# A list of 128 indices loaded as one run and turned onto the partitions by TensorE, with 2 MB instead of 1.5 MB of x loaded ahead of a gather

## The reference, cut to what matters

```python
# x: (128, 64, 512) float32, 16.8 MB
# itok_B_0_7: (128,) int32 in 0..7; itok_B_1_198: (128,) int32 in 1..198
# L0_cond_weights: (8, 64, 64); L1_cond_weights: (200, 64, 64)
w = L0_cond_weights[itok_B_0_7]
x = x + einsum('bct,bcd->bdt', x, w)
w = L1_cond_weights[itok_B_1_198]
x = x + einsum('bct,bcd->bdt', x, w)
return x
```

## Time and profile before

| | us |
|---|---|
| median of 3 runs | 92.57 (92.44 to 92.94) |
| the profiled execution | 92.7 |
| its span, first to last instruction | 90.8 |
| TensorE busy | 76.8 (85%) |
| VectorE busy | 60.0 (66%) |
| ScalarE busy | 57.0 (63%) |
| bytes moved by DMA | 35.93 MB, mean 396 GB/s |

### The profile page before, as it was taken

The page is one execution under the profiler, slowest core; times in us unless marked ns, Lnnn a source line. Parts: engine busy times, 40 slices in busy tenths (PEclk is TensorE's granted clock), DMA queues, the critical chain, the costliest instruction groups (busy, mean ns, idle before and its releaser), DMA issues.

```text
span 90.8 us, 2458 instructions
## 1 busy us (share of the span) xinstructions
PE 76.8 (85%) x906; PEld 42.9 (47%) x906; DVE 60.0 (66%) x124; ACT 57.0 (63%) x114; POOL 23.5 (26%) x119
## 2 busy tenths in 40 slices
PE   0599959977999999999999999999999999992000
PEld 0489749965545443544544454454444444440000
DVE  1096019994388787978878788888787887887000
ACT  2899807885367675867776677777576775775000
POOL 3400049989998988000000000000000000000000
PEclk9999999999999999999999999999999999999755
DMA  0999999999999999999999999999999999999992
GB/s 6 337 446 424 455 361 415 420 399 409 409 413 402 409 418 394 419 418 424 411 415 426 415 413 420 420 422 420 411 415 422 420 419 428 404 424 420 419 399 103
DMA packets 9453, 35.93 MB, mean 396 GB/s; under 512 B 737, under 2 KB 866, under 8 KB 9314
## 3 DMA queue, kind: packets, MB, share of 16 engines
q1 hardware_dynamic: 4512, 16.78, 46.1%
q10 hardware_dynamic: 4786, 16.91, 45.8%
q0 software_dynamic: 144, 2.10, 5.4%
HBM read 19.01 MB, written 16.78 MB: 394 GB/s over the span
## 4 chain that ended last, share of the span: by engine, by line
PE 68%; DMA 12%; DVE 9%; issue 1%; DVEq 1%; ACTq 0%; POOLq 0%
PE psum L225 58%; DMA w_rows<-in_L_cond_weights_dram,cond 10%; DVE w L269 7%; PE psum L206 7%; PE psum L247 2%; DMA subjects<-in_itok_B_dram 2%; DVEq L75 1%; PE psum L186 1%; DVE xy L303 1%; ACTq L370 0%; DVE m_diag L276 0%; DVE w_rows L365 0%; POOLq L155 0%; DVEq L275 0%
## 5 line engine op out<-in xcount | busy, mean ns | idle before, releaser
L225 PE MATMUL psum<-xy,m_diag 64*128 64x512 f32 x240 | 53.4, 595 | 0.0
L303 DVE COPY xy<-psum 64x512 f32<-64x512 f32 x60 | 41.0, 684 | 11.1 <-PE psum L225 10.2
L303 ACT COPY xy<-psum 64x512 f32<-64x512 f32 x60 | 34.9, 582 | 17.5 <-PE psum L225 16.8
L225 PEld LDWEIGHTS psum<-xy,m_diag 64*128 64x128 f32 x240 | 22.6, 187 | 25.6 <-issue 25.0
L163 POOL COPY w0b<-w0t 64x64 f32 x112 | 21.7, 237 | 10.1 <-DMA w_rows<-in_L_cond_weights_dram,cond 8.2
L206 PEld LDWEIGHTS psum<-w,w0b 64*32 64x32 f32 x512 | 5.6, 105 | 6.4 <-issue 3.0
L269 ACT COPY w<-psum 64x256 f32<-64x256 f32 x16 | 5.8, 365 | 3.8 <-PE psum L186 2.8
L186 PE MATMUL psum<-ident,w_rows 128*64 128x128 f32 x64 | 7.2, 274 | 1.0 <-DVE w_rows L365 1.0
L378 ACT COPY w<-w_rows 128x256 f32<-128x256 f32 x18 | 7.3, 405 | 0.8 <-DMA w_rows<-in_L_cond_weights_dram 0.2
L186 PEld LDWEIGHTS psum<-ident,w_rows 128*64 128x64 f32 x64 | 7.0, 151 | 1.3 <-DVE w_rows L365 1.3
L206 PE MATMUL psum<-w,w0b 64*32 64x64 f32 x512 | 6.9, 224 | 0.9 <-DVE w L269 0.9
(11 more groups left out here) (14 smaller groups left out, 7.2 us busy)
## 6 DMA issues: line engine op xcount, KB each, us to landing
xy<-in_x_dram SPq DMA_DIRECT2D x15, 1024.0 KB, 19.7
out_dram<-xy ACTq DMA_DIRECT2D x14, 1024.0 KB, 14.4
out_dram<-xy ACTq DMA_DIRECT2D x4, 512.0 KB, 8.3
xy<-in_x_dram SPq DMA_DIRECT2D x2, 512.0 KB, 5.8
w_rows<-in_L_cond_weights_dram ACTq DMA_DIRECT2D x1, 128.0 KB, 2.5
cond<-in_itok_B_dram SPq DMA_DIRECT2D x1, 0.5 KB, 2.2
subjects<-in_itok_B_dram ACTq DMA_DIRECT2D x1, 0.5 KB
w_rows<-in_L_cond_weights_dram,cond POOLq DMA_INDIRECT x1, 9.2
```

Source lines behind the costliest of these rows:

```text
L225: last = nc.tensor.matmul(psum[:, 2 * (s % Y_RING) + h, :], m_diag[rows, odd, v % M_RING, j, :], xy[rows, s, j * T:(j + 1) * T], start=j = ...
L303: copy(xy[rows, s, i * T:(i + 1) * T], psum[HALVES[i], 2 * (s % Y_RING) + h, :]).then_inc(done, 1)
```

## The change

The index list is loaded as one run of 512 bytes into one partition, `cond_row`. VectorE converts its 128 integers to floats, TensorE transposes the row of floats into a column of PSUM (128 partitions, one value each), and VectorE converts that column back to integers in `cond`, on which the gather waits. SP issues 2 MB of x instead of 1.5 MB before its wait, in two loads of 1 MB; the second was two loads of 0.5 MB, with the wait between them.

```diff
+        cond_row = sb("cond_row", [1, B], i32)
+        cond_float = sb("cond_float", [1, B], fp32)
         cond = sb("cond", [B, 1], i32)
...
+        cond_psum = psum[:, 6, 0:1]
...
-            sp.dma_start(cond[:, :], cond_dram.rearrange("(b o) -> b o", o=1)).then_inc(s_cond, 16)
+            sp.dma_start(cond_row[:, :], cond_dram.rearrange("(o b) -> o b", o=1)).then_inc(s_cond_row, 16)
             load(0, 2)
-            load(2, 1)
+            load(2, 2)
 
             sp.wait_ge(s_w0b_early, EARLY * UNIT)
-            load(3, 1)
             for v in range(2, UNITS):
                 load(2 * v, 2)
...
-            pool.wait_ge(s_cond, 16)
+            pool.wait_ge(s_cond, 1)
             nc.gpsimd.indirect_dma_start(
...
             pe.wait_ge(s_ident, 1)
+            pe.wait_ge(s_cond_float, 1)
+            nc.tensor.transpose(cond_psum, cond_float[:, :], ident[0:1, 0:1]).then_inc(s_cond_turned, 1)
+
             pe.wait_ge(s_w0_rows, 16)
...
-                    pe.wait_ge(s_x[v], 32 if v == 1 else 16)
+                    pe.wait_ge(s_x[v], 16)
...
+            dve.wait_ge(s_cond_row, 16)
+            nc.vector.tensor_copy(cond_float[:, :], cond_row[:, :]).then_inc(s_cond_float, 1)
+            dve.wait_ge(s_cond_turned, 1)
+            nc.vector.tensor_copy(cond[:, :], cond_psum).then_inc(s_cond, 1)
+
             dve.wait_ge(s_ident, 1)
             dve.wait_ge(s_subjects, 16)
             dve.wait_ge(s_w0_turned, 1)
```

More of the change, by code:

```diff
@@ L95, in bass_cond_residual_kernel @@
         w0_psum = psum[0:C, 7, :]
+        cond_psum = psum[:, 6, 0:1]
+        s_cond_row = sem("s_cond_row")
+        s_cond_float = sem("s_cond_float")
+        s_cond_turned = sem("s_cond_turned")
         s_cond = sem("s_cond")
```

## The result

The changed kernel takes 93.53 us (median of 6 runs, 93.15 to 94.34) against 92.70 (6 runs, 92.44 to 92.94). The ratio is 1.0105, with a 95% interval of 1.0058 to 1.0152: it is slower, by 0.8 us at the median. I had forecast no change, 92.6 in a range of 92.0 to 93.1. In what follows, four slow runs of the experiment e3 (94.06 to 94.54 us) are left out of its median and its ratio.

What follows compares the result with a forecast made beforehand. The prediction took the DMA engines to bind the kernel. Start 0.0, crossing 0.0 and TensorE 1.3 us later but hidden left the span at 90.8 us, a median of 92.6 us, range 92.0 to 93.1.

Steps and rivals of the forecast that it cites:

- the cover: At the last store: TensorE and the copies may come up to 3.1 us later before the end moves.
- Step 1: Load of the index list at the start: 0.0 us taken, bounds -0.74 and +0.16.
- Step 2: Chain from cond to the gather: gather starts at 3.85 instead of 3.26, 0.6 us later, hidden by x.
- Step 3: 0.52 MB more x ahead of the gather: 1.28 us more, gather lands at 13.7 instead of 12.42.
- Step 4: Work behind the gather: 1.3 us later, TensorE ends at 83.6, hidden by the cover of 3.1 us.
- third rival: TensorE becomes the bound, over 3.1 us late through its clock or shared engines: 94.4 or 93.9 us; chance 0.05.
- Step 5: Two 0.5 MB loads of x made into one of 1 MB, and three semaphores: costs nothing.
- second rival: Gather ready only after x is through at 8.0 us, engines idle: 0.1 to 0.7 us slower; chance 0.06.

Runs made afterwards that it cites:

- e3: Changed kernel, with the x loads behind SP's wait held until ScalarE's 15th copy, about 9.6 us instead of 8.0; 93.17 us, ratio 1.0049.
- e8: e2 with only 1 MB of x ahead of SP's wait instead of 1.5 MB; 93.90 us, ratio 1.0123 to the kernel before.
- e7: Kernel before, with 10 of ScalarE's unread copies and their TensorE transposes instead of 18; 96.89 us, ratio 1.0419.
- e2: Changed kernel's one-run load of cond, but 1.5 MB of x ahead of SP's wait as before; 92.65 us, ratio 0.9984 to the kernel before.
- e10: e2 with 21 unread copies (filler work for TensorE) instead of 18; 92.73 us, ratio 0.9986 to the kernel before.
- e4: Changed kernel with 25 unread copies, each followed by three TensorE transposes, instead of 18; 92.83 us, ratio 1.0009 to the kernel before.
- e9: e1 with 25 unread copies instead of 18; 92.85 us, ratio 1.0006 to the kernel before.
- e1: Kernel before, with 2 MB of x ahead of SP's wait and cond loaded as before; 94.39 us, ratio 1.0148.

## Why the prediction was wrong

*What bounds the kernel, and the cover.* Right. That the DMA engines bind, that the last store needs 3.5 us alone, and that TensorE may be 3.1 us late came out of two rows, and all kernels of the table but e8 follow it, e7 with the reserve above. The last store of the changed kernel took 3.5 us to land.

*Step 1, the start.* The sum took 0.0. SP's issue of the run took 0.34 us and not the 0.54 I had copied from subjects; the engines filled about 0.3 us earlier (194 GB/s instead of 63 from 1.5 to 2.5 us is 0.13 MB), inside my bounds, and e2 shows no measurable gain from it.

*Step 2, the chain to the gather.* Right in kind, too dear in size: 0.21, 0.23 and 0.16 us for the three operations, where I had 0.15, 0.41 and 0.15, and the run landed at 2.0 and not 2.75. The gather started at 3.08, below my lower bound of 3.3. In e8 and e10, with the same load, it started at 3.46 and 3.50, since the conversion began only at 2.4, so this term alone scatters by 0.4 us.

*Step 3, the landing of the gather.* This step failed. I had +1.28, from 0.52 MB at 410 GB/s, and it is +2.31 (14.73 instead of 13.7, outside the 13.4 to 14.0 that I had called right). The 0.52 MB were priced well: the last gather packet starts 1.39 later. What I put at nothing, without a reason, is the tail: that packet took 0.66 longer and its landing 0.25 longer. Nor did I allow for the scatter of the landing, 0.6 us among the kernels with 1.5 MB ahead. I also read "q0 alone for 4 us" as a rule that the queues follow one another, and wrote that no packet of the x issued at 8 us ran before the gather was through. Both were too wide: even before, such packets ran from 11.56 us, beside gather packets that ended at 12.03, and with 2 MB ahead q1 and q0 ran side by side from 7.3 us on. Here the page of the Trainium skill that I had set against the trace ("DMA: Bandwidth & Descriptors", Queues, rings and completion order: an engine takes turns between the queues that have work) agrees with the trace of the changed kernel, with 76 packets of q1 beside 96 of q0. It does not for the x issued at 8 us, which had no packet before 11.5 in either kernel; why is not shown.

*Step 4, what follows the gather.* It failed with step 3. I reckoned 2.3 us of idle time and a clock that holds, because it had held for nearly 3 us after the last matmul. With the idle time at 3.59 us it did not: the 64 transposes took 1.66 us longer. Nor were those 3 us a safe length, since in e7 the clock fell after 2.58 us; whether it would have held after 2.3 no run shows. So the lateness is 2.31 + 1.66 = 3.97 instead of 1.3, and 3.97 - 3.1 = 0.87 shows at the end. This is the third rival, to which I gave 0.05. I had priced the clock's fall closely there, at 1.8 us against 1.66 measured, and with the 1.3 us it came to just the cover. What went over it is the 1.0 us by which the gather landed later still, and I had let the two stand as unlikely one by one, though they have one source: the late landing lengthens the idle time, and with it the clock fell. The late gather alone is hidden: e4 and e9 keep it, take away the clock's part, and lose nothing. That the clock's fall with a landing only 1.3 us late would be hidden too (1.3 + 1.66 = 2.96, under 3.1) is an estimate, and no run shows it.

*Step 5 and the second rival.* The merged loads cost nothing that shows. The gap before the gather did not come, as forecast. Nothing had shown me how soon a gather is ready, and I allowed 3.4 us from its start; in e8 its first packet came 1.85 us after it (5.31 against 3.46), so this rival had less for it than I gave.

## What to carry to other kernels

Where one resource binds and another follows close behind, work out the slack of the second from the last transfer (its time to landing, less what it takes alone), and then add up every way in which the change makes the second one late: here the 1.3 us of extra data grew to 4.0, by 1.0 until the gather had landed and 1.7 through TensorE's clock. Putting more bulk data ahead of a transfer that a chain waits for is free only while that sum stays below the slack. Filler work that keeps TensorE busy must cover most of the wait (1.90 us left idle did no harm here, 2.58 did); when a change makes the wait longer, the filler has to grow with it (25 copies in place of 18 gave back the loss here). And a landing time read from one execution carries its scatter, here 0.6 us, into every sum built on it.

## What the runs showed of the hardware that I had not expected

TensorE's clock fell to half (0.50 in the rows, which is 1.2 GHz) around idle times of 3.59 us (changed), 3.28 (e1), 3.11 (e3) and 2.58 (e7), and stayed at 1.00 with 1.90 us (e2) and less. By the clock records it fell before the work began again in e1 (at 13.9 us, the transposes at 15.04) and 0.9 us after it in the changed kernel (15.9 and 15.03). The 2.58 us are shorter than the nearly 3 us that I had taken from the end of the run before as safe.

A load of 512 bytes as one run could be read by VectorE at 1.99 us, 1.24 us after its issue, in the changed kernel, at 2.0 in e2, e3 and e4, and at 2.4 in e8 and e10; the same bytes on 128 partitions took 2.2 us to land.

The same 64 transposes took 7.22 us at the full clock in six kernels, and 8.59 to 9.94 with part of them at the lower one (e3, e7, changed, e1). The times of the changed kernel and of e1, with such a fall, spread over 1.2 and 1.35 us, those of e4 and e9, without one, over 0.3 and 0.55.
